# Low halves of the down weights moved behind the gate multiplication and ahead of the up multiplication, their transforms moved to other steps

## The reference

```python
def _L0_attn_ref(x, Wq, Wk, Wv, Wo):          # 32 query heads of 16, 8 key/value heads
    ...
    attn = jnp.einsum('bhqd,bhkd->bhqk', q, k) * scale
    attn = jax.nn.softmax(attn, axis=-1).astype(jnp.float16)
    out = jnp.einsum('bhqk,bhkd->bhqd', attn, v)
    ...
    return out @ Wo

def _L0_ffn_ref(input, SU_ug, SU_dp, Wscale_ug, Wscale_dp, W_up, W_gate, W_down):
    ...
    x = fwht(x * SU_ug) / SCALE                # Walsh-Hadamard transform, 512 long
    x_up = x @ W_up.T * (Wscale_ug[:INTER] * SCALE)
    x_gate = x @ W_gate.T * (Wscale_ug[INTER:] * SCALE)
    x = jax.nn.silu(x_gate) * x_up
    x = fwht(x * SU_dp) / SCALE                # 2048 long
    x = x @ W_down.T * (Wscale_dp * SCALE)
    return x.reshape(input.shape)

xn = _layernorm(x, axis=-1)
s = _L0_attn_ref(xn, ...)
g = _silu(_L0_ffn_ref(xn, ...))
x = x + s * g
```

## Time and profile before

| | |
|---|---|
| Time, median of three | 1347.81 us |
| Profiled execution: its time, its span | 1347.46 us, 1345.6 us |
| Busy over the span: PE, PEld, DVE, ACT, POOL | 93%, 48%, 78%, 58%, 40% |
| The 16 transforms | from 174.0 to 236.5 us |
| Busy in 171 to 242 us: PE, DVE, ACT | 61.47, 52.67, 49.21 us of 71 |

### The profile page before, as it was taken

One profiled execution on the slowest core, in us unless ns is written; L12 is line 12 of the kernel. 1 busy time (PEld: TensorE's weight loads), 2 busy tenths in 40 slices (PEclk: granted clock), 3 DMA queues, 4 the chain that ended last, 5 costly groups with the idle time before them and its releaser, 6 DMA issues. The chain is left out here.

```text
span 1345.6 us, 23533 instructions
## 1 busy us (share of the span) xinstructions
PE 1245.6 (93%) x8738; PEld 643.4 (48%) x8738; DVE 1050.6 (78%) x1823; ACT 785.1 (58%) x1306; POOL 542.1 (40%) x466
## 2 busy tenths in 40 slices
PE   5877888999999999999779999999999999999998
PEld 2332333334434443443334547755586546855475
DVE  6788886888888888899847886697686885878855
ACT  4775776678867887788366543365234652365431
POOL 3599962113312330233023743157331762237431
PEclk9899999999999999999889999999999999999999
DMA  6664654787788768877970213102401024002121
GB/s 232 222 154 90 104 96 84 140 160 136 124 147 169 137 119 155 165 141 123 222 289 32 54 30 72 40 8 61 92 4 48 13 60 84 17 32 55 38 33 48
DMA packets 344002, 135.59 MB, mean 101 GB/s; under 512 B 312177, under 2 KB 331345, under 8 KB 341329
## 3 DMA queue, kind: packets, MB, share of 16 engines
q1 hardware_dynamic: 329424, 126.22, 43.2%
q0 software_dynamic: 2048, 6.29, 1.5%
q10 hardware_dynamic: 12416, 1.57, 1.1%
HBM read 44.87 MB, written 17.87 MB: 47 GB/s over the span
## 5 line engine op out<-in xcount | busy, mean ns | idle before, releaser
L1182 PE MATMUL bank<-rows,both 128*128 128x512 f16 x1024 | 237.5, 381 | 5.9 <-DVE both L639 2.7
L958 ACT ACTIVATE probs<-vpair,top_n 128x512 f16<-128x512 f32 x256 | 170.0, 686 | 121.1 <-DVE top_n L650 114.3
L650 DVE TENSOR_REDUCE top_n<-vpair 128x1 f32<-128x512 f32 x256 | 169.9, 685 | 61.1 <-PE bank L1151 61.1
L1196 PE MATMUL bank<-dn,h 128*128 128x512 f16 x768 | 181.6, 384 | 0.0
L958 ACT ACTIVATE probs<-bank,top_n 128x512 f16<-128x512 f32 x256 | 164.3, 688 | 0.0
L650 DVE TENSOR_REDUCE top_n<-bank 128x1 f32<-128x512 f32 x256 | 163.7, 681 | 0.0
L1182 PEld LDWEIGHTS bank<-rows,both 128*128 128x128 f16 x1024 | 94.8, 98 | 128.9 <-issue 16.3
L455 POOL TENSOR_TENSOR h<-th,h 128x512 f16<-128x512 f32 x61 | 70.5, 1156 | 155.6 <-ACT h L927 155.4
L2263 PE MATMUL bank<-rows,both 128*128 128x512 f16 x512 | 117.2, 379 | 0.0
L1196 PEld LDWEIGHTS bank<-dn,h 128*128 128x128 f16 x768 | 71.5, 99 | 93.3 <-issue 17.6
L2279 PE MATMUL bank<-both,hid 128*128 128x512 f16 x512 | 111.2, 379 | 0.0
(11 more groups left out here) (359 smaller groups left out, 2602.8 us busy)
## 6 DMA issues: line engine op xcount, KB each, us to landing
h<-in_ug SPq DMA_DIRECT2D x8, 1024.0 KB, 6.4
lt_scratch<-big SPq DMA_DIRECT2D x16, 384.0 KB, 2.7
dn<-in_down SPq DMA_DIRECT2D x2, 2048.0 KB, 11.5
x_scratch<-th POOLq DMA_DIRECT2D x16, 256.0 KB, 4.0
res<-x_scratch SPq DMA_DIRECT2D x16, 256.0 KB, 4.1
out_x<-res SPq DMA_DIRECT2D x16, 256.0 KB, 2.0
both<-in_w SPq DMA_DIRECT2D x2, 1548.0 KB, 8.6
t_scratch<-tok SPq DMA_DIRECT2D x16, 192.0 KB, 2.1
```

What stands on the lines that cost most here:

```text
L650: v.tensor_reduce(top_n[:, i:i + 1], SC_[n % G][:, :], AX.X, ALU.max, negate=True).then_inc(S["max_done"], 1)
L958: a.activation(probs[:, k % TAKEN, j * T:(j + 1) * T], SC_[j][:, :], ACT.Exp, bias=top_n[:, i:i + 1]).then_inc(S["p_ready"], 1)
L1182: mm = pe.matmul(GB[n % 2][:, :], w[:, kt, col:col + P], xnb(b, kt), start=r == 0, stop=r == 2 * KT - 1)
L1196: mm = pe.matmul(bk, h16(ft, r // 2)[:, rows], dn16(ft, r % 2), start=j == 0 and r == 0, stop=j == FT - 1 and r == 2)
```

## The change

The steps of the transforms are changed, and in VectorE's code the low half moves: that of an even step behind the next step's first maximum and gate multiplication, that of an odd step ahead of the up multiplication. The transforms of steps 53, 61 and 62 go; 56, 64 and 69 are added. Steps 53 and 61 have a projection, and so has 69. No instruction is added or taken away, and the orders of GpSimd and SyncE are the same.

```diff
-DN_AT = (49, 51, 52, 53, 55, 57, 58, 59, 60, 61, 62, 63, 65, 66, 67, 68)
+DN_AT = (49, 51, 52, 55, 56, 57, 58, 59, 60, 63, 64, 65, 66, 67, 68, 69)
...
                 p, r = divmod(t - PREP, 4)
-                if t % 2 and t - 1 in DN_AT:
-                    low_down(DN_AT.index(t - 1))
                 if r == 2 and 0 <= p < NCH:
                     take_sum(p)
...
                 if b < B and m > FFN_STEP and m % 2:
                     gate_mul(b, (m - FFN_STEP) // 2)
+                if t % 2 and t - 1 in DN_AT:
+                    low_down(DN_AT.index(t - 1))
                 if paired:
                     for j in range(1, G):
                         row_max(G * (ta // 2) + j)
                 if t % 2 and 0 <= (t - 3 - FFN_STEP) // 2 < LOW_FIRST:
                     low_rows((t - 3 - FFN_STEP) // 2)
+                if t % 2 and t in DN_AT:
+                    low_down(DN_AT.index(t))
                 if b < B and m > FFN_STEP and m % 2:
                     up_mul(b, (m - FFN_STEP) // 2)
-                if t % 2 and t in DN_AT:
-                    low_down(DN_AT.index(t))
```

## The result

The changed kernel takes 1342.30 us (median of 8 runs, 1339.74 to 1344.56) against 1348.25 for the kernel before (8 runs on the same chip): a ratio of 0.9951, with 0.9936 to 0.9966 at 95%. Two later comparisons gave 0.9947 (0.9927 to 0.9967) and 0.9953 (0.9934 to 0.9971). The medians alone differ by 5.95 us (0.9956). The forecast was 1343.1, and it counted every gain under 0.5%, 6.7 us, as "same". The measured change of 0.49% lies right at that bound and has the forecast sign. None of the three intervals reaches 1, so the gain is real; the forecast gain of 4.6 us is on the small side of it.

A forecast was written before the change was run, and what follows sets the result against it. No engine is full; a loop through TensorE, ScalarE and VectorE sets the time. Gains 7.10 (steps 53, 61) and 0.74 (six others), less 2.30 (step 69) and 0.98 (step 55), give 4.56: 1343.1 us, range 1339.5 to 1347.5.

The forecast's parts named there:

- the projections of 53 and 61: TensorE's projections in steps 53 and 61 wait 0.2 us in place of 2.3; both steps together gain 7.10 us.
- step 69 takes back: The query projection of step 69 newly waits 1.7 us behind the transform added there, costing 2.30 us.
- step 55 takes: Step 54's token transpose, reciprocal and division on VectorE delay step 55's first maximum; the pair loses 0.98 us.
- The unknown price: On VectorE, a low half behind a gate multiplication, not shown before: between 8.6 us faster and 3.7 us slower.
- the walk's value: Following hand-overs through TensorE, ScalarE and VectorE, pairs from step 51 to 71 sum to 60.17 us, gain 4.56.
- the new wait is covered: Odd transforms wait about 0.75 us for the bank, covered since ScalarE takes the high half only at scores plus 4.00.
- rival C: Odd high halves pass scores plus 4.00, delaying ScalarE's exponentials; seven pairs lose 8.3 us in all: 1351.5 us; chance 0.04.
- Rival A: All TensorE waits vanish and step 69 hides its projection: gain 6.9 to 8.6 us, 1340.0 us; chance 0.13.
- B: Missed small waits of 0.3 to 0.5 us in most pairs give gain back: 1.3 us left, 1346.4 us; chance 0.15.
- D: Total unchanged, as ScalarE and VectorE later use the time to wait for transposed probabilities: 1347.5 us; chance 0.06.
- curable only by a second bank: TensorE's waits for the one PSUM bank need another bank; otherwise gain stays near 4.6 us, by order alone 8.6.
- outside the stretch nothing moves: Only the 71 us, about 5% of the kernel, holding the changed steps gets shorter, through an earlier start of step 71's scores.

The follow-up runs named there:

- one maximum later: Changed kernel with an even step's low half behind the second maximum too; 65.48 us between scores of steps 51 and 71, ratio to before 0.9986.
- both further edits: Changed kernel with an even step's low half ahead of the gate multiplication and step 69's transform moved to step 48; 1339.15 us, ratio to before 0.9933.
- steps only: Kernel before with only the new list of transform steps, VectorE's order kept; ratio to before 0.9970.
- odd behind up: Changed kernel with an odd step's low half put back behind the up multiplication; ratio to before 0.9960.
- step 48: Changed kernel with step 69's transform moved to step 48 and one GpSimd pair a step earlier; 1339.21 us, ratio to before 0.9925.
- order only: Changed kernel with the transform steps of the kernel before, so only VectorE's order is changed; ratio to before 0.9990.

## Why the prediction was right

**The mechanism and the sum.** The length of every pair came within 0.06 us of the forecast, and the sum within 0.13 (60.04 against 60.17), so no large errors cancelled. The gain in the stretch is 4.69, forecast 4.56. The parts are right as well: the projections of 53 and 61 give 3.13 and 3.99 (7.10 forecast for both), step 69 takes back 2.29 (2.30), step 55 takes 0.95 (0.98). Each size came from the distance between starts in the trace of before, not from busy times, and the operations that were moved (the small ones of step 54 as well) were walked in their new order. These small ones do hold up step 55, whose scores are at 189.46: its first maximum starts 0.98 behind them (forecast 1.02).

```profile
190.10 0.42 DVE L702 TENSOR_TENSOR otok<-oblk,rl 128x256 f16<-128x256 f32 x1
190.44 0.68 DVE L650 TENSOR_REDUCE top_n<-vpair 128x1 f32<-128x512 f32 x1
```

Two places of the working are not as they should be. Pair 51 is 5.68 in it, but its own numbers, a transform at 181.71 and 1.06 to the scores, give 5.71, which is what was measured. And the 0.72 from a maximum to its exponential and the 0.81 from the fourth exponential to the scores are put down to the earlier trace rows, which show no exponential; the trace of before has the first (204.50 to 205.21) and for the second 0.73 to 0.83.

**The unknown price.** A low half behind a gate multiplication was bounded between 8.6 faster and 3.7 slower. It came out at the walk's value, its start at 2.01 to the hundredth. The wait for tanh is 0.29 in brackets and 0.37 by starts (1.40 against 1.03), where the text had said 0.4; that of the odd transform in step 59 is 0.58 in brackets and 0.74 by starts (0.75).

**What the forecast put as "the new wait is covered"** is shown by the run with one maximum later: 0.6 more exposes 0.6. The rival C, slower, was decided at 4.00 against 3.97, and the case did stand just on the good side. Rival A fell with the wait of 1.57 at step 69, B with pairs within 0.06, D with the three timed comparisons and with the first profiles, where the second layer starts 3.2 us earlier after the scores of step 71 had come 3.5 earlier.

**What was wrong beside it.** The prediction inferred that these waits are curable only by a second bank, and that with one bank the gain stays near 4.6 us and not at 8.6. The kernel with both further edits has the one bank and, by order and steps alone, is 8.5 us shorter than before between the scores of 49 and 71. Its waits ahead of the projections are gone, and those ahead of transforms are 1.1 us in all.

**The size in timed runs.** The ratios of the three comparisons say 6.6, 7.1 and 6.3 us (0.9951, 0.9947, 0.9953 of 1347.5), the stretch 4.7, which is 0.9965: inside all three intervals, but near the end of each. What may be too small is the term "outside the stretch nothing moves", together with the clock of 1.00 in the stretch, taken from one profile. What the runs show in its place: in one of four profiles of before the wait of 2.3 us at step 53 was followed by a fall of the clock that cost 1.69 more, and none of the changed kernel's three has such a fall in the stretch. A shorter wait is no guarantee, since the kernel with one maximum later lost the same 1.7 behind a wait of 1.57. In six of the seven experiments the ratio says more than the trace too (steps only 4.0 us against 2.2, odd behind up 5.4 against 2.9, step 48 10.1 against 6.9). The seventh is order only, the one that still waits 1.57 at steps 53 and 61 (1.3 against 2.1). That fits a loss of clock behind the waits of before, but it is not shown: these profiles don't settle how often such a fall comes, and where the rest of the timed gain lies stays open.

## What to carry to other kernels

When one bank of PSUM, the memory that matmuls write to, is handed round three engines, write down for each engine the start of every operation after a common event, and walk it through with start-to-start distances from the trace: that gave a sum right to 0.13 us in 60. An instruction that frees a shared bank should stand as early in its engine's row as its own input allows, ahead of one that still has to wait (here ahead of the gate multiplication, 1.3 us), but not ahead of work whose input is there sooner (at the head of the row it held up the first maximum; behind the gate it gained 0.8 us). Work that occupies the bank should be kept out of steps in which another user of it follows (2.2 us for the one transform of step 69, its new place in step 48 counted). Where an engine's wait has been covered exactly, look for what the cover ends in before moving anything later: one instruction more cost its full 0.6 us in each of the pairs 57 and 59.

## What had not been expected of the hardware

A wait on TensorE can be followed by a fall of its clock, and then more is lost than the wait. After 2.30 us idle at step 53 the granted clock fell to 0.50, the 1.2 GHz level, for about 3 us in one of four executions of the kernel before; the eight matmuls behind the projection then took 3.25 us in place of 1.89, and 1.7 us were lost. After 1.57 us idle at step 69 the same came in the one profile of the kernel with one maximum later. The same waits in the other executions left the clock at 1.00: of the eight waits of 2.3 us ahead of a projection in the four profiles of before, one was followed by a fall, and of nine waits of 1.57 to 1.71 us in the other kernels, one. What decides it, no run here shows.

The start of an execution scatters too. The time of step 49's scores, which all these kernels but the two with step 48 reach by the same instructions, lies between 169.5 and 173.0 us, and the granted clock in 20 to 40 us is 0.83 to 1.00 in those profiles. The first row is of the changed kernel (scores of step 49 at 172.61), the second of the kernel with the odd low half behind up (169.53):

```profile
20.00:40.00 20.00, 15.24 (x32) 6.91 (x33) 9.80 (x27) 13.47 (x23) 7.13 (x4) 0.83 0.70 256
```

```profile
20.00:40.00 20.00, 14.47 (x37) 6.27 (x38) 11.66 (x29) 13.78 (x23) 9.09 (x4) 1.00 0.69 259
```

The two profiles with a clock of 1.00 there are the two earliest, but the nine with 0.91 alone spread from 170.9 to 173.0, so the clock of this stretch is at most a part of it. The scatter of 3.5 us ahead of step 49 is more than most of the single edits here are worth; that is why the pairs of steps were compared and not the spans.
